# Fused group norm and attention: where the first four value units stand, and how the last two tiles are finished

## The reference

```python
h = group_norm(x, gn_w, gn_b)
hf = h.reshape(Bn, Cn, Hn * Wn)
q = jnp.einsum('bcn,oc->bno', hf, wq) + bq
k = jnp.einsum('bcn,oc->bon', hf, wk) + bk[None, :, None]
v = jnp.einsum('bcn,oc->bno', hf, wv) + bv
alpha = jnp.einsum('bnc,bcm->bnm', q, k) / jnp.sqrt(jnp.float32(Cn))
alpha = jax.nn.softmax(alpha, axis=-1)
out = jnp.einsum('bnm,bmc->bnc', alpha, v)
out = jnp.einsum('bnc,oc->bon', out, wo) + bo[None, :, None]
return out.reshape(Bn, Cn, Hn, Wn) + x
```

## Time and profile before

| | |
|---|---|
| median of 3 runs | 220.31 us |
| the runs | 219.82, 220.31, 221.62 us |
| the profiled execution | 219.72 us |
| its span in the trace | 218.0 us |
| outside the span | 1.72 us |

### The profile page before, as it was taken

The page is one execution under the profiler, slowest core; times in us unless marked ns, Lnnn a source line. Parts: engine busy times, 40 slices in busy tenths (PEclk is TensorE's granted clock), DMA queues, the critical chain, the costliest instruction groups (busy, mean ns, idle before and its releaser), DMA issues.

```text
span 218.0 us, 4306 instructions
## 1 busy us (share of the span) xinstructions
PE 203.2 (93%) x1513; PEld 140.7 (65%) x1513; DVE 180.5 (83%) x277; ACT 176.4 (81%) x279; POOL 165.9 (76%) x233
## 2 busy tenths in 40 slices
PE   1898698979999999999999999999998999999993
PEld 0774274637766776767676776777675766766992
DVE  2668997898889899889889888989877888788742
ACT  2448999798898889998898889888998789888820
POOL 6038898567699999999589967899699999796410
PEclk9999999999999999999999999999999999999999
DMA  5790999999999999999999999999999999999994
GB/s 155 226 410 28 173 163 206 188 184 166 239 179 214 193 195 224 238 180 204 218 161 240 192 197 228 207 197 207 247 158 227 194 223 211 181 179 220 213 371 152
DMA packets 135029, 44.61 MB, mean 205 GB/s; under 512 B 131168, under 2 KB 131936, under 8 KB 135008
## 3 DMA queue, kind: packets, MB, share of 16 engines
q1 hardware_dynamic: 134432, 44.08, 104.1%
q10 hardware_dynamic: 576, 0.26, 0.5%
HBM read 7.61 MB, written 4.22 MB: 54 GB/s over the span
## 4 chain that ended last, share of the span: by engine, by line
PE 81%; DMA 5%; DVE 4%; issue 3%; ACT 3%; SPq 2%; POOL 1%; DVEq 0%; POOLq 0%
PE O L607 12%; PE O L609 11%; PE O L608 11%; PE S L580 11%; PE S L576 11%; PE S L578 11%; DMA pT<-parts 3%; PE M L472 3%; PE M L474 3%; PE M L473 3%; DMA bo_sb<-in_L_conv_bo_dram 3%; DVE neg_logits L917 2%; ACT S L785 1%; DVE parts L933 1%; ACT parts L796 1%
## 5 line engine op out<-in xcount | busy, mean ns | idle before, releaser
L917 DVE TENSOR_SCALAR_CACHE_REDUCE neg_logits<-S,c_tok 128x1024 f32<-128x1024 f32 x64 | 81.9, 1280 | 19.8 <-PE S L580 19.4
L785 ACT ACTIVATE S<-neg_logits,exp_bias 128x1024 f32<-128x1024 f32 x64 | 71.5, 1118 | 12.9 <-DVE neg_logits L917 12.3
L933 DVE SCALAR_TENSOR_TENSOR parts<-S,parts 128x1024 f16<-128x1024 f32 x64 | 78.1, 1220 | 3.3 <-ACT parts L796 2.8
L607 PE MATMUL O<-pT,v_hi 128*128 128x256 f16 x240 | 65.4, 272 | 2.4 <-ACT av L765 1.4
L796 ACT ACTIVATE parts<-S 128x1024 f16<-128x1024 f32 x64 | 65.4, 1022 | 1.8
L609 PE MATMUL O<-pT,v_lo 128*128 128x256 f16 x240 | 65.4, 273 | 0.0
L608 PE MATMUL O<-pT,v_hi 128*128 128x256 f16 x240 | 65.4, 272 | 0.0
L576 PE MATMUL S<-h_hi,u_hi 128*128 128x512 f16 x128 | 38.1, 379 | 1.7 <-DVE parts L933 1.7
L580 PE MATMUL S<-h_hi,u_lo 128*128 128x512 f16 x128 | 38.1, 379 | 0.0
L578 PE MATMUL S<-h_lo,u_hi 128*128 128x512 f16 x128 | 38.1, 379 | 0.0
L607 PEld LDWEIGHTS O<-pT,v_hi 128*128 128x128 f16 x240 | 24.4, 102 | 8.1 <-issue 3.3
(11 more groups left out here) (148 smaller groups left out, 288.0 us busy)
## 6 DMA issues: line engine op xcount, KB each, us to landing
x_sb<-in_x_dram SPq DMA_DIRECT2D x7, 512.0 KB, 8.3
inv_rows<-inv_line SPq DMA_DIRECT2D x6, 512.0 KB, 4.5
out_dram<-x_sb SPq DMA_DIRECT2D x6, 512.0 KB, 4.8
pT<-parts SPq DMA_TRANSPOSE x62, 4.9
out_dram<-x_sb SPq DMA_DIRECT2D x3, 256.0 KB, 3.9
x_sb<-in_x_dram SPq DMA_DIRECT2D x2, 256.0 KB, 3.2
out_dram<-x_sb SPq DMA_DIRECT2D x2, 128.0 KB, 2.5
inv_line<-row_inv SPq DMA_DIRECT2D x6, 4.0 KB, 2.3
```

What stands on the lines that cost most here:

```text
L607: nc.tensor.matmul(o, vh, ph, start=(m == 0), stop=False)
L785: nc.scalar.activation(S[T % 3][:, :], neg_logits[:, n % 2, :], ACT.Exp, scale=-1.0, bias=exp_bias[:, p, n:n + 1], accum_out=row_sum[:, p, ...
L917: nc.vector.tensor_scalar(neg_logits[:, n % 2, :], S[T % 3][:, :], c_tok[:, p, n:n + 1], None, ALU.add, ALU.min, accum_out=exp_bias[:, p, ...
L933: nc.vector.scalar_tensor_tensor(out=parts[:, T % SPLITS, N:2 * N], in0=S[T % 3][:, :], scalar=P_SCALE, in1=parts[:, T % SPLITS, 0:N], op0 ...
```

## The change

- `LEAD` goes; `FIRST_UNITS` names the tiles of the first group's units: unit 0 at T = 5, 1 at T = 6, 2 at T = 8 and 3 at T = 9. T = 7 and T = 10 have none. All other units stay at their tiles.
- The copy of the first group's sums stands ahead of the exponentials of T = 10 on ACT, not behind them. For b >= 2 the order stays.
- The last pair of tiles is no longer done as one piece of 256 columns but as two of 128: 24 products for tile 62 into half of `S[1]`, 24 for tile 63 into half of `S[2]`, each behind the copies of its own tile's transpose. DVE's last multiplication, addition and SP's store follow for each tile, so that there are four pieces (512, 256, 128 and 128 columns) in place of three.

```diff
-    LEAD = 5
+    FIRST_UNITS = {5: 0, 6: 1, 8: 2, 9: 3}
...
-        LAST = (slice(0, GT // 2), slice(GT // 2, GT))
-        LAST_COLS = (slice(0, GN), slice(GN, GN + GN // 2), slice(GN + GN // 2, N))
+        LAST = (slice(0, 2), slice(2, 3), slice(3, 4))
+        LAST_BANKS = (M[:, :], S[1][:, HALF:N], S[2][:, 0:HALF])
+        LAST_COLS = (slice(0, GN),) + tuple(slice(GN + t.start * 128, GN + t.stop * 128) for t in LAST)
...
-            past = T - (LEAD if T < LEAD + GT else LAG)
+            past = FIRST_UNITS.get(T, T - LAG)
...
-            def last_values(half):
-
-                bank = (M, S[1][:, HALF:N])[half]
-                if half == 0:
+            def last_values(i):
+
+                if i == 0:
...
-                    pe.wait_ge(last_tr_hi, 2)
-                    pe.wait_ge(last_tr_lo, 2)
+                    pe.wait_ge(last_tr_hi, i)
+                    pe.wait_ge(last_tr_lo, i)
...
-                    o = bank[:, 0:GN // 2]
+                    o = LAST_BANKS[i][:, 0:(LAST[i].stop - LAST[i].start) * 128]
...
-                    if LEAD <= TILES * b + n < LEAD + GT or TILES * b + n >= LAG + GT:
+                    if TILES * b + n in FIRST_UNITS or TILES * b + n >= LAG + GT:
                         values(*unit_of(b, n))
...
-            for half in range(2):
-                last_values(half)
+            for i in range(len(LAST)):
+                last_values(i)
...
+                    if n == 2 and b == 1:
+                        copy_values(0, 0)
                     if n == 6 and b >= 1:
                         copy_values(b - 1, 1)
                     exponentials(b, n)
-                    if n == 2 and b >= 1:
+                    if n == 2 and b >= 2:
                         copy_values(b - 1, 0)
                     high_part(b, n)
...
-            for i, (cols, bank) in enumerate(zip(LAST_COLS, (O, M, S[1][:, HALF:N]))):
+            for i, (cols, bank) in enumerate(zip(LAST_COLS, (O[:, :],) + LAST_BANKS)):
```

More of the change, by code:

```diff
@@ L622, in last_values @@
                     pe.wait_ge(lo_done, TILES * B - 2)
-                    pe.wait_ge(last_tr_hi, 2)
-                    pe.wait_ge(last_tr_lo, 2)
+                    pe.wait_ge(last_tr_hi, i)
+                    pe.wait_ge(last_tr_lo, i)
                 for m in range(TILES):
                     vh, vl = v_hi[:, (B - 1) % 3, m, 0:C], v_lo[:, (B - 1) % 3, m, 0:C]
-                    ph, pl = (pT[:, (2 * B - 1) % PT, part * TILES + m, LAST[half], :].rearrange("p t n -> p (t n)")
+                    ph, pl = (pT[:, (2 * B - 1) % PT, part * TILES + m, LAST[i], :].rearrange("p t n -> p (t n)")
                               for part in range(2))
-                    o = bank[:, 0:GN // 2]
+                    o = LAST_BANKS[i][:, 0:(LAST[i].stop - LAST[i].start) * 128]
                     nc.tensor.matmul(o, vh, ph, start=(m == 0), stop=False)
```

## The result

| | before | after |
|---|---|---|
| median of 20 runs each | 221.16 us | 219.84 us |
| lowest to highest | 218.87 to 223.33 us | 217.75 to 224.5 us |
| the profiled execution | 219.72 us | 219.35 us |
| its span | 218.0 us | 217.6 us |

After stands to before as 0.9939, interval [0.9912, 0.9966]: 1.3 us faster, 0.6%, where 217.6 us and a gain of 2.3 were forecast. A second comparison, on another chip, gave 0.9925 [0.9886, 0.9965]. Single executions of one kernel lie 4.5 us apart and more, so the traces are compared stage by stage and not by their ends.

What follows compares the result with a forecast made beforehand. PE, busy 93% of the span, was taken as the bound, with 2.8 us idle ahead of 47.5 us. 219.72 - 2.0 (loop) - 0.3 (end) = 217.4, named as 217.6 for a median; own range 216.8 to 218.3, 8 in 10 for 216.7 to 219.2.

Steps and rivals of the forecast that it cites:

- may lie as far above again: Level: profiled execution lies 0.6 below the runs' median, 220.31; a new median may lie that far above again; 217.6 named.
- the tail: End of the kernel, last pair by single tiles: 0.3 us gained; 0 to 0.7 in the forecast's own range.
- part 3: End by single tiles: PE's last product stays, DVE saves 0.25 us, last store 0.1; sum 0.3 (0 to 1.5).
- Part 1: First group's units at 5, 6, 8, 9: sums copied at 43.7, unit 4 at 44.4; loop gains 2.0 us.
- Part 2: Copy of the sums ahead of T = 10's exponentials on ACT; up to 0.3 of the 2.0 us may go.
- its 0.2 us of cover: T = 10: high part out at 46.5, DVE free at 46.7; without this cover up to 0.3 us is lost.
- rival 3: Last pair: 128-column products wait for weights, 0.11 apart, 2.6 us later: 220.0, by half 218.7; chance 0.04.
- Everything behind it keeps its order, and today PE runs there without idle but for 0.63: Loop behind the first group, 47.5 to 214.6 us: order unchanged, PE nearly never idle, so the 2.0 us gain stays.
- rival 1: DMA queue: late-loop transposes don't come forward with PE, so it waits: 218.5 to 219.1 us; chance 0.14.
- rival 4: POOL has no slack at inverses and `h_lo`; inverses landing later would delay PE: 221.9 us; chance 0.06.

Runs made afterwards that it cites:

- end alone: Kernel before with only the last pair of tiles done as single tiles, loop unchanged: 220.52 us, 0.9995 [0.9952, 1.0039].
- new order: Kernels with the first group's units at T = 5, 6, 8 and 9, as in after: 219.84 us, 0.9939 against before.
- old order: Kernels with the first group's units at T = 5 to 8, as in before: 221.16 us.
- loop alone: Kernel before with the changed units and the earlier copy of the sums, end unchanged: 219.27 us, 0.992 [0.9879, 0.9961].
- late stores: SP's stores of images 0 to 2 moved from the loop to behind the last transpose: on after 218.84 us, 0.9908; on before 219.32 us, 0.9936.
- units alone: Kernel before with the units at T = 5, 6, 8 and 9, copy of the sums not moved: 221.42 us in one execution.

## Why the prediction was wrong, step by step

**The level: 1.2 us of the 2.2.** The forecast set out from the profiled execution, 219.72, and added 0.2 for the median. The median of 20 runs of before was 221.16, 1.44 above that execution and 0.85 above the median of three that was shown. The term "may lie as far above again" was mis-sized by 1.2. The other 1.0 of the miss is the change's effect: 1.3 us in place of 2.3. The stated range also counted the tail as 0 to 0.7 where part 3 had given 0 to 1.5; the result lies on the other side of it.

**Part 1: right, its dates to 0.3 us.** After starts 0.18 earlier than before, so the dates of the prediction are to be read 0.18 earlier. Timelines of PE, then of ACT, in after:

```profile
34.02 0.38 PE L577 MATMUL S<-h_hi,u_hi 128*128 128x512 f16 x1
...
44.08 0.27 PE L608 MATMUL O<-pT,v_hi 128*128 128x256 f16 x1
...
47.82 0.38 PE L492 MATMUL M<-mv,neg_mean_mat 128*128 128x1 f32 x2 [0.98 <-DVE mv L871]
...
55.23 0.38 PE L577 MATMUL S<-h_hi,u_hi 128*128 128x512 f16 x1
```

```profile
43.24 0.62 ACT L765 ACTIVATE av<-O 128x512 f32<-128x512 f32 x1
```

The logits of T = 8 follow those of T = 7 without the wait of 1.04. The copy of the sums starts at 43.24 (43.5 by the forecast and the start), unit 4 at 44.08 (44.2), group_mean at 47.82 (47.9) behind a wait of 0.98 for DVE (1.1). From T = 3 to 15 PE gains 2.00 us, and 2.0 was forecast.

**Part 2: right.** The copy's place was worth 0.16, and no loss of its 0.2 us of cover shows.

**Part 3: right in its terms, and covered by the new wait.** The end of after, timelines of PE and DVE:

```profile
209.31 0.27 PE L630 MATMUL M<-pT,v_hi 128*128 128x256 f16 x1 [1.90 <-DMA pT<-parts]
...
214.56 0.22 PE L632 MATMUL S<-pT,v_lo 128*128 128x128 f16 x1
```

```profile
214.88 0.29 DVE L1024 SCALAR_TENSOR_TENSOR attn_last<-S,last_inv 128x128 f32<-128x128 f32 x1 [0.72 <-PE S L632]
215.21 0.29 DVE L1028 TENSOR_TENSOR x_sb<-attn_last,x_sb 128x128 f32<-128x128 f32 x1
```

DVE's last two operations take 0.29 each (0.3 forecast, 0.42 in the earlier trace rows). From DVE's end to the span's is 2.1 us, where before had 2.4: the store gave 0.3, not 0.1. Products of 128 columns stand 0.056 apart (24 of them from 211.93 to 213.27), so rival 3 falls. The 81 ns of the Trainium skill ("TensorE: Matmul & The Clock Gate", Back-to-back issue gap) don't hold for this stream. Where no wait stands ahead, the stage from T = 63 to the end takes 17.53 after and 18.00 or 18.06 before: 0.5 us, against 0.3. In after's first trace the 1.90 at L630 covers it more than three times over. The end alone, with the same wait, shows no gain in time.

**The step that failed: "Everything behind it keeps its order, and today PE runs there without idle but for 0.63".** PE ran there without idle, but with next to no slack towards SP's queue. PE's logits came forward by 2.0; the transposes and the inverses of the row sums, which stand in that queue, did not. From the logits of T = 3 to the issue of tile 41's transpose are 126.78 and 125.38 us in two traces of before, 124.94 and 125.64 in two of after, 126.47 in the loop alone. POOL waits 9.6 to 10.8 us for the inverses in the traces of the new order with SP's stores in the loop, 5.3 to 8.5 in the old. How this reaches PE, by the timelines of POOL and PE, in before and then in the loop alone:

```profile
131.97 1.52 POOL L408 TENSOR_TENSOR attn<-av,inv_rows 128x512 f32<-128x512 f32 x1 [2.58 <-DMA inv_rows<-inv_line]
...
140.06 1.16 POOL L346 TENSOR_TENSOR h_lo<-h,h_hi 128x512 f16<-128x512 f32 x1
...
141.93 0.38 PE L472 MATMUL M<-h_hi,wu_hi 128*128 128x512 f16 x1
```

```profile
131.47 1.53 POOL L408 TENSOR_TENSOR attn<-av,inv_rows 128x512 f32<-128x512 f32 x1 [3.92 <-DMA inv_rows<-inv_line]
...
139.56 1.15 POOL L346 TENSOR_TENSOR h_lo<-h,h_hi 128x512 f16<-128x512 f32 x1
...
140.86 0.38 PE L472 MATMUL M<-h_hi,wu_hi 128*128 128x512 f16 x1 [1.22 <-POOL h_lo L346]
```

Counted from the logits of T = 3, these inverses land at 110.70 in before and 110.66 in the loop alone (109.8 to 110.7 in the three traces of the old order, 108.9 to 110.7 in those of the new one with SP's stores in the loop), and `h_lo` ends 9.4 us later in both, at 120.09 and 120.04. PE got there at 120.80 in before, 0.7 behind `h_lo`; in the loop alone it gets there 1.1 ahead of it. In after with late stores the inverses land at 104.97, `h_lo` ends at 114.36, and PE starts at 118.78 without a wait.

From 23 to 63 four traces of the new order with SP's stores in the loop (after twice, loop alone, units alone) take 119.04 to 120.47, mean 119.9, the three of the old order 118.03 to 118.82, mean 118.3: 1.5 us of the 2.0 come back here in these traces. No trace has a wait of PE on a transposed tile in this stage; the waits are those on `h_lo` at T = 43 and 51, and in some traces one of 0.3 for DVE at T = 45. With the three stores gone or late they are gone, and the stage is 118.0 to 118.2: so the load of these stores brings them, in the traces. At the end the last pair meets tile 61 still under way, in both orders, as told above.

In time this account is not confirmed in full. With late stores, where the stage gives nothing back, the new order gains 1.0 us (0.3 to 1.7), no more than the 1.3 of the change with its stores in place. Where the rest of the 2.0 goes over many runs stays open.

Two rivals had a part of this. The cause is that of rival 1, weighed at 0.14, a queue that does not come forward with PE; the place at which PE pays in the loop is that of rival 4, weighed at 0.06 (POOL and `h_lo`), at a far smaller price than its 221.9; only the wait at the end stands where rival 1 had it. Rival 1's time of 218.5 to 219.1, taken from 219.72, is a gain of 0.6 to 1.2; 1.3 was measured. What spoke against rival 1 was the earlier trace rows: SP waits for DVE's low part at 51 transposes. That row was misread. The wait ahead of tile 41's transpose in before, by the waits of SP's queue in 147.90 to 147.94 us:

```profile
SPq L241 <- DVE parts L933: 1.0, 1, 1.0
```

It is put down to a low part, but tile 41's had ended at 141.62, 6.3 us before; the one that ended within this issue, at 148.84, is tile 43's. Where the work that a transpose needs was done long ago, something else held the queue. Three views could have told so: the low parts' ends beside the transposes' issues (42 of 62 in before go out over 1 us behind their low part, 18 in after with late stores); SP's own timeline, where a transpose of T = 23 to 61 holds the queue for 2.74 us on the mean and PE takes 2.97 a tile; and the last columns of the earlier trace rows, a DMA share of 1.13 at 211 GB/s. They were signs of a second bound close beside PE's, and I took the lines for PE's columns alone.

## What to carry to other kernels

An idle gap removed early in a pipeline pays only as far as every other queue can follow; where a second resource is nearly as full as the first, ask what its next date is and whether that date moves too. Read a queue's wait against the end of the work that it names: one that was done microseconds before is not what ended the wait. When single executions scatter by more than the change, compare stages between fixed points of the program, and give the level of the forecast the spread of the runs, not the luck of one profile.

## What the runs showed of the hardware

- Stores issued by ACT delayed the transposes as much as stores issued by SP: tile 41's lag is 6.4 us in the one trace with three stores of 512 KB on ACT's queue, 4.8 to 8.0 in the traces with them on SP's, and 0.4 to 2.9 with them moved behind the transposes.
- The same transpose, tile 1's, at the same place in the program, lands in 4.4 to 4.7 us in 14 traces and in 6.2 or 6.3 in two.
- The stores of the last pieces land later when more runs beside them: 64 KB in 1.6 us and 128 KB in 1.9 in after's first trace, 2.4 and 2.6 with late stores.
- Tile 61's transpose lands in 4.3 to 5.0 us in ten traces and in 6.3 to 6.5 in six; PE waits for it in these six alone. What makes it so is not shown.
